# Attention: the copy of a head's sums ahead of the row parts on VectorE

## What is computed

```python
qkv = x @ attn_qkvw + attn_qkvb              # x is layernorm(x), 32 heads of 32 features
q, k, v = ...                                # (batch, head, row, feature)
scores = jnp.einsum('bhqd,bhkd->bhqk', q, k) * scale
probs = jax.nn.softmax(scores, axis=-1)
ctx = jnp.einsum('bhqk,bhkd->bhqd', probs, v)
...
return ctx @ attn_ow + attn_ob
```

## Time and profile before

| | us |
|---|---|
| median of 3 executions | 3279.01 |
| lowest, highest | 3276.21, 3280.91 |
| the profiled execution | 3280.28 |
| its span, first to last instruction | 3278.5 |
| first and last copy of sums (L754) | at 119.7, at 1850.7 |

### The profile page before, as it was taken

One profiled execution on the slowest core, in us unless ns is written; L12 is line 12 of the kernel. 1 busy time (PEld: TensorE's weight loads), 2 busy tenths in 40 slices (PEclk: granted clock), 3 DMA queues, 4 the chain that ended last, 5 costly groups with the idle time before them and its releaser, 6 DMA issues. The chain is left out here.

```text
span 3278.5 us, 62409 instructions
## 1 busy us (share of the span) xinstructions
PE 3153.2 (96%) x24128; PEld 1718.0 (52%) x24128; DVE 2264.4 (69%) x3904; ACT 1744.8 (53%) x2125; POOL 1937.3 (59%) x2062
## 2 busy tenths in 40 slices
PE   5999999999999999999999899998999999999999
PEld 2455555555555555555444455555466666665344
DVE  7777777777777777777878587776466666653622
ACT  4667777777777777767677422222245555552000
POOL 3577777777777777777677422221466666650522
PEclk9999999999999999999999799999999999999999
DMA  6122222222222222222344644453222333224642
GB/s 222 45 67 63 78 63 74 63 77 66 72 66 72 66 72 67 71 64 68 98 129 123 196 161 161 160 163 117 103 84 103 110 107 112 97 84 156 244 154 96
DMA packets 286055, 344.11 MB, mean 105 GB/s; under 512 B 92225, under 2 KB 215105, under 8 KB 285762
## 3 DMA queue, kind: packets, MB, share of 16 engines
q1 hardware_dynamic: 281090, 323.33, 31.3%
q10 hardware_dynamic: 4608, 16.78, 1.3%
q0 software_dynamic: 64, 0.01, 0.0%
HBM read 200.95 MB, written 138.55 MB: 104 GB/s over the span
## 5 line engine op out<-in xcount | busy, mean ns | idle before, releaser
L727 DVE TENSOR_REDUCE nmax<-ring_ps 128x1 f32<-128x512 f32 x1024 | 676.4, 685 | 387.0 <-PE ring_ps L486 384.3
L887 POOL TENSOR_TENSOR elo<-e,ehi 128x1024 f16<-128x1024 f32 x256 | 669.2, 2614 | 358.8 <-ACT ehi L629 358.8
L623 ACT ACTIVATE e<-st_ps,exp_scale 128x1024 f32<-128x1024 f32 x512 | 570.7, 1115 | 378.9 <-PE st_ps L496 315.6
L537 PE MATMUL proj_ps<-xnT,arena 128*128 128x512 f16 x3024 | 738.8, 380 | 23.2 <-DVE arena L829 23.2
L629 ACT ACTIVATE ehi<-st_ps,exp_scale 128x1024 f16<-128x1024 f32 x512 | 568.5, 1110 | 0.0
L1642 PE MATMUL f_ps<-wT,fxT 128*128 128x512 f16 x1920 | 435.7, 380 | 2.9 <-DMA fxT<-xT_scratch 2.9
L537 PEld LDWEIGHTS proj_ps<-xnT,arena 128*128 128x128 f16 x3024 | 267.8, 97 | 300.3 <-DVE arena L829 23.6
L486 PE MATMUL ring_ps<-ks,qs 96*128 96x512 f16 x1024 | 398.8, 390 | 20.2 <-DVE nmax L727 19.2
L496 PE MATMUL st_ps<-qs,ks 98*128 98x512 f16 x1024 | 393.9, 385 | 11.0 <-ACT ehi L629 10.9
L513 PEld LDWEIGHTS ctx_ps<-v_sb,ehi 128*128 128x128 f16 x4096 | 313.0, 98 | 155.1 <-DVE sums L754 39.2
L513 PE MATMUL ctx_ps<-v_sb,ehi 128*128 128x65 f16 x4096 | 372.7, 192 | 12.5 <-DVE sums L754 11.2
(11 more groups left out here) (233 smaller groups left out, 4695.8 us busy)
## 6 DMA issues: line engine op xcount, KB each, us to landing
qk_scratch<-qk_hl SPq DMA_DIRECT2D x128, 256.0 KB, 2.3
fxT<-xT_scratch SPq DMA_DIRECT2D x64, 512.0 KB, 3.5
qs<-qk_scratch SPq DMA_DIRECT2D x192, 128.0 KB, 2.6
ks<-qk_scratch SPq DMA_DIRECT2D x192, 128.0 KB, 2.9
arena<-x_scratch SPq DMA_DIRECT2D x48, 512.0 KB, 4.4
ctx_scratch<-ctx SPq DMA_DIRECT2D x64, 256.0 KB, 3.2
xb<-in_L_attn_a_x_dram SPq DMA_DIRECT2D x32, 512.0 KB, 4.4
x_scratch<-xb SPq DMA_DIRECT2D x32, 512.0 KB, 2.6
```

The lines of the kernel that those rows point to most:

```text
L537: mm = pe.matmul(bank(u), wqk(g, qk, wp, c), xnT[:, b % 2, xp, c, :], start=(n == 0), stop=(n == 23))
L623: nc.scalar.activation(e32[:, half], st_ps[:, half], ACT.Exp, scale=exp_scale[:, 0:1]).then_inc(e32_done, 1)
L727: dve.tensor_reduce(nmax[:, h % 2, c:c + 1], ring_ps[:, ring_max(h, c) % 2, :], AX.X, ALU.max, negate=True).then_inc(ring_free, 1)
L887: nc.gpsimd.tensor_tensor(elo[:, h % 2, 2:4, :], e32[:, 1], ehi[:, h % 2, 2:4, :], ALU.subtract).then_inc(elo_pool, 1)
```

## The change

`leave_ctx` moves on VectorE from sub-slot 0 of a slot into sub-slot 3 of the slot ahead of it, behind the maximum and ahead of `row_parts`. As the slot is an earlier one, its argument is s - 2 instead of s - 3: the head is the same.

```diff
                         for s in SLOTS:
                             for c in range(T):
                                 if c == 0:
-                                    leave_ctx(s - 3)
                                     lo_exps(s - 1)
                                 max_of(s + 2, c)
                                 if c == T - 1:
+                                    leave_ctx(s - 2)
                                     row_parts(s + 2)
```

## The result

The changed kernel takes 3262.5 us (median of 4, 3258.2 to 3264.4), the kernel before, on the same chip, 3280.0 us (median of 4, 3276.2 to 3281.7). The ratio is 0.9942, with a 95% interval of 0.9930 to 0.9954: 17.5 us faster, where 13.2 were forecast. The time lies in the stated range of 3254 to 3274.

A forecast was written before the change was run, and what follows sets the result against it. TensorE was taken to set the pace in the attention. Terms of 4.0 us (25 statistics slots), 7.3 us (two collisions) and 1.9 us (first statistics slot) made 13.2 us off 3279.0: 3265.8 us, range 3254 to 3274.

The forecast's parts named there:

- The 25 waits go, at no cost for the new place: Statistics slots: the copy ends 0.42 us behind the slot's last maximum, not 1.68, so TensorE's 25 waits for sums go.
- Rival D: GpSimd holds VectorE's copy of the sums as it holds L735; 25 x 0.1 = 2.5 us slower, 3281.5 us; chance 0.02.
- part three: Slot behind each statistics slot: L745 is held again and the ring matmul waits for the maximum; only 4.0 us gained.
- part four: Collisions of L745 with GpSimd's L887: two go as L745 asks 0.4 us earlier, 7.3 us; first statistics slot, 1.9 us.
- The first statistics slot: Near 128 us, L745 would start ahead of L887 and end 2.1 us earlier; 1.9 us taken for TensorE.
- Rival B: Behind statistics slots, L735 asks before GpSimd's cast and L745 precedes L942: 10 us more gain, 3255.5 us; chance 0.18.
- E: Nothing measurable: the 0.44 us goes to the next slot, other executions lack the collisions; 3277 to 3281 us; chance 0.09.
- F: Slower: the reciprocal holds VectorE's queue until TensorE's context matmuls end, so L745 follows L887; +63 us, 3342; chance 0.04.

The follow-up runs named there:

- The first experiment: Kernel before, with reciprocal and copy behind the row parts and ahead of the second half of the statistics, in the 26 statistics slots only: 3263.3 us, ratio 0.9947.
- the other-slots run: Kernel before, with the change in all slots but the 26 with statistics, which keep the order of before: 3270.5 us, ratio 0.9966.
- e6: Changed kernel, with two tiny VectorE writes ahead of each L745 in all slots: 3256.4 us, ratio 0.9926.
- e10: Changed kernel, with the two tiny VectorE writes ahead of L745 in the 26 statistics slots alone: 3254.3 us, ratio 0.9918.

## Why the prediction was right, and where it was off

- *The 25 waits go, at no cost for the new place.* Right. The reciprocal starts ahead of R, the copy ends at R + 0.41, and it takes 0.40 us beside GpSimd's L942 or L901; the longest of all 256 is 0.40. In 249 heads it ends 0.40 or 0.41 us behind the maximum; in the other seven, all in the last heads, the reciprocal waits for TensorE. Rival D is out. The page of the Trainium skill that the prediction names for D says of copy that it can contend, where its operands meet conditions, so these durations do not contradict the page as the prediction had it.
- *The wait turns into one for the maximum in the next slot, and 4.0 of 12 us stay* (part three). Right in its mechanism, with L735 0.08 us behind the cast where 0.05 had been reckoned, and L745 held to 2.19 us where 1.78 stood. The term was too small: 5.4 us. The wait is 0.36 instead of 0.4 us.
- *Collisions* (part four). How a collision works and that the change gives L745 more room was confirmed by the delay on the kernel before (31 collisions, 3.7 us each) and by its harmlessness on the changed one. The term of 7.3 us for two measured 7.6. I had overlooked a third, near 484 us, of 1.1 us. But that these three went because of the room is not shown, and it may be luck. The trace before has five pauses of VectorE put down to "issue", of 0.20 to 0.27 us, ahead of L753 or L754 (170.0, 479.3, 1091.3, 1397.9 and 1711.7 us); counted in VectorE's rows of the trace, waits on semaphores included, they lie 512 or a multiple of it apart. The changed kernel, with other instructions at these places, has none of them, so its room was never put to this trial. The first experiment lost the collision near 1402 us with its pause and without the room. What makes the pauses stays open. The first statistics slot gave 2.1 where 1.9 stood.
- *No term for the end of the attention.* The sum had left this out. Between the heads 216 and 248 TensorE gains 4.7 us and gives 2.9 back behind them: 1.8 net of the 5.4 us by which the 18.6 exceed the 13.2. The 25 slots (5.4 for 4.0) and the collisions (8.7 for 7.3) are 1.4 each. There are no statistics slots in these heads, and the other-slots run, with the same orders there, gains 2.5, so the amount hangs on how the engines arrive. The largest part are four waits, in the heads 229, 233, 237 and 241. Before, a maximum stood behind an L790 (part of a weight of the output projection) there and the ring matmul waited 0.61 to 0.85 us for it, as here on VectorE and TensorE:

```profile
1661.29 1.21 DVE L745 TENSOR_TENSOR elo<-e,ehi 128x1024 f16<-128x1024 f32 x1
1662.43 0.68 DVE L727 TENSOR_REDUCE nmax<-ring_ps 128x1 f32<-128x512 f32 x1
1663.03 2.55 DVE L790 SCALAR_TENSOR_TENSOR xt<-xt,so 128x1024 f16<-128x1024 f32 x1
...
1666.24 0.41 PE L486 MATMUL ring_ps<-ks,qs 96*128 96x512 f16 x1 [0.61 <-DVE nmax L727]
```

With the new order these four waits are gone in the changed kernel and in the other-slots run, 2.7 us. I had not looked at them.
- *Rival B* had a chance of 0.18 and did not come in the changed kernel, but it did in three other kernels: e1, where reciprocal and copy stand behind the row parts and ahead of the statistics, and e6 and e10, with the delay. That 0.05 us decide was said; that they decide over some 8 to 9 us of a change worth 17 was seen only here.
- *Rivals E and F.* The time is outside both. No reciprocal waited for TensorE between 187 and 1494 us; the few of the last heads come behind that.

## What to carry to other kernels

Where an instruction of one engine is held for the whole of another engine's, look in the trace at who asks first and by how much: 0.1 us of margin is worth more than 0.1 us of work. Moving an instruction ahead on one engine shifts every later meeting with the other, so a gain in one slot must be followed to the end of the next. And when one engine's order has changed, check the order of the engine that it meets as well; here that was worth some 11 us of 29. When a rare event is gone after a change, look whether the change prevented it or only moved what set it off.

## What the runs showed that I had not expected

Added work made the kernel faster: two writes of 0.07 us in 26 slots took 8.2 us off. The same two writes in all slots of the kernel before cost 98.8 us. Of VectorE instructions that follow each other at once, the second was not held by a GpSimd instruction that started beside it: behind the held L738, L745 took 1.21 us and L942 was held to 2.1 to 2.2 us. And a matmul wait of 2 us was mostly followed by a lower clock: the granted clock is 0.56 from 1402.50 to 1405.50 us before, so most of it at 1.2 GHz and not 2.4 (six matmuls of 512 columns in 2.59 us in place of 1.46), and the collision costs 3.7 us where the wait alone is 2.1. It did not always follow. Behind the wait of 2.11 us near 784 us in the first experiment the granted clock stays 1.00 (780 to 787 us), and that collision cost 2.3 us.
